# Two first projections back to back on TensorE, and the down weights' high part behind the copies of the sums on ScalarE

## The reference

```python
x = L0_attn_x                                    # (1, 2048, 512) float32
xn = _layernorm(x, axis=-1)
s = _L0_attn_ref(xn, Wq, bq, Wk, bk, Wv, bv)     # q: 16 x 32 heads, k and v: 16 x 8 heads
g = _silu(_L0_ffn_ref(xn, ln_w, gate_w, up_w, down_w))
x = x + s * g

# in _L0_ffn_ref (inner size 1792)
nx = x * jax.lax.rsqrt(mean(square(x)) + RMS_EPS) * ln_w
g = jnp.einsum('bsh,ih->bsi', nx, gate_w)
u = jnp.einsum('bsh,ih->bsi', nx, up_w)
return jnp.einsum('bsi,hi->bsh', jax.nn.silu(g) * u, down_w)
# in _L0_attn_ref, for each token by itself, between its 16 rows d and e
scores = jnp.einsum('bsdh,bseh->bsde', q, k) / sqrt(16)
out = jnp.einsum('bsde,bseh->bsdh', softmax(scores), v)
```

## Time and profile before

| | |
|---|---|
| median of 3 runs | 473.84 us (473.63 to 474.03) |
| the profiled execution's own time | 474.23 us |
| its span, first to last instruction | 472.4 us |
| PE busy | 465.8 us (99%) |
| DVE, ACT, POOL busy | 411.9 (87%), 243.7 (52%), 120.7 us (26%) |
| granted TensorE clock | 1.000, full speed (2.4 GHz) |

### The profile page before, as it was taken

The page is one execution under the profiler, slowest core; times in us unless marked ns, Lnnn a source line. Parts: engine busy times, 40 slices in busy tenths (PEclk is TensorE's granted clock), DMA queues, the critical chain, the costliest instruction groups (busy, mean ns, idle before and its releaser), DMA issues.

```text
span 472.4 us, 6230 instructions
## 1 busy us (share of the span) xinstructions
PE 465.8 (99%) x2130; PEld 391.6 (83%) x2130; DVE 411.9 (87%) x559; ACT 243.7 (52%) x417; POOL 120.7 (26%) x104
## 2 busy tenths in 40 slices
PE   8999999999999999999999999999999999999997
PEld 7899888888888878888888888888888888888886
DVE  6999778987898997989989898999998888888994
ACT  4784665568588888654112545225225335358102
POOL 2920213116221122233443101000011111127920
PEclk9999999999999999999999999999999999999999
DMA  8606997579779996573474649546656655514772
GB/s 269 253 2 239 356 370 263 224 263 259 213 246 307 291 369 248 188 268 133 135 231 167 218 188 366 207 182 223 222 201 223 223 200 201 200 44 135 288 247 89
DMA packets 44623, 105.70 MB, mean 224 GB/s; under 512 B 20272, under 2 KB 21808, under 8 KB 41264
## 3 DMA queue, kind: packets, MB, share of 16 engines
q1 hardware_dynamic: 44592, 105.31, 63.5%
HBM read 69.90 MB, written 35.40 MB: 223 GB/s over the span
## 4 chain that ended last, share of the span: by engine, by line
PE 95%; POOL 2%; DVE 1%; DMA 1%; ACT 0%; issue 0%; SPq 0%; POOLq 0%; DVEq 0%
PE gu_ps L558 18%; PE gu_ps L560 18%; PE gu_ps L561 18%; PE y_ps L700 8%; PE y_ps L701 8%; PE y_ps L702 8%; PE gu_ps L702 3%; PE gu_ps L700 3%; PE gu_ps L701 3%; PE gu_ps L729 2%; PE gu_ps L728 2%; PE gu_ps L733 2%; DMA xz<-x 1%; POOL h_kept L514 0%; PE y_ps L742 0%; PE gu_ps L579 0%
## 5 line engine op out<-in xcount | busy, mean ns | idle before, releaser
L558 PE MATMUL gu_ps<-z_hi,w_ops 128*128 128x512 f32 x378 | 147.2, 389 | 0.0
L560 PE MATMUL gu_ps<-z_lo,w_ops 128*128 128x512 f32 x378 | 147.1, 389 | 0.0
L561 PE MATMUL gu_ps<-z_hi,w_ops 128*128 128x512 f32 x378 | 147.1, 389 | 0.0
L501 POOL TENSOR_TENSOR h_lo<-h,h_hi 128x512 fp32r<-128x512 f32 x28 | 36.8, 1315 | 229.3 <-ACT h_hi L930 229.2
L558 PEld LDWEIGHTS gu_ps<-z_hi,w_ops 128*128 128x128 f32 x378 | 70.9, 188 | 15.2 <-ACT u L905 0.5
L561 PEld LDWEIGHTS gu_ps<-z_hi,w_ops 128*128 128x128 f32 x378 | 71.0, 188 | 14.8
L560 PEld LDWEIGHTS gu_ps<-z_lo,w_ops 128*128 128x128 f32 x378 | 70.9, 188 | 14.6
L700 PE MATMUL y_ps<-wd_ops,h_hi 128*128 128x512 f32 x168 | 65.6, 390 | 0.0
L701 PE MATMUL y_ps<-wd_ops,h_hi 128*128 128x512 f32 x168 | 65.5, 390 | 0.0
L702 PE MATMUL y_ps<-wd_ops,h_lo 128*128 128x512 f32 x168 | 65.5, 390 | 0.0
L930 ACT ACTIVATE h_hi<-h 128x512 fp32r<-128x512 f32 x28 | 17.6, 630 | 58.8 <-DVE h L1229 58.7
(11 more groups left out here) (143 smaller groups left out, 750.1 us busy)
## 6 DMA issues: line engine op xcount, KB each, us to landing
w_kept<-w_ops SPq DMA_DIRECT2D x13, 1792.0 KB, 6.4
w_ops<-w_kept SPq DMA_DIRECT2D x13, 1792.0 KB, 7.6
wd_ops<-wd_kept SPq DMA_DIRECT2D x35, 512.0 KB, 4.2
raw<-gate_up SPq DMA_DIRECT2D x30, 256.0 KB, 4.3
wd_kept<-wd_ops SPq DMA_DIRECT2D x14, 512.0 KB, 7.5
xz<-x SPq DMA_DIRECT2D x16, 256.0 KB, 6.0
raw<-down SPq DMA_DIRECT2D x14, 256.0 KB, 7.8
w_ops<-wd_kept SPq DMA_DIRECT2D x7, 512.0 KB, 7.0
```

The source lines that it names most:

```text
L501: pool.tensor_tensor(lo, src, hi.bitcast(F32), ALU.subtract).then_inc(h_lo_done, 1)
L558: pe.matmul(acc, w_h, z_hi[:, zi, c, :], start=start and c == 0, stop=False, skip_group_check=True)
L560: pe.matmul(acc, w_h, z_lo[:, zi, c, :], start=False, stop=False, skip_group_check=True)
L561: end = pe.matmul(acc, w_l, z_hi[:, zi, c, :], start=False, stop=c == 1, skip_group_check=True)
```

## The change

It adds and removes no instruction. It moves these, in the front of the program and in the groups 1 to 13 of the first pair:

```diff
@@ block.sync (SP)
             load_x(0, (JJ - 1,))
+            load_down(0)
             load_gate(1)
             load_up(1)
-            load_down(0)
             load_down(1)
@@ block.gpsimd (POOL)
             scale_tile(J)
+            scale_tile(J + 1)
             pool.wait_ge(bias_in, 48)
...
-            for j in range(J + 1, JJ):
-                scale_tile(j)
+            scale_tile(J + 2)
+            scale_tile(J + 3)
@@ block.tensor (PE)
             qkv_product(0)
+            qkv_product(1)
             second_tile(J)
-            qkv_product(1)
             second_tile(J + 1)
+            qkv_product(2)
             second_tile(J + 2)
-            qkv_product(2)
             second_tile(J + 3)
             qkv_product(3)
             gate1(0)
@@ block.scalar (ACT), the front
             z_tile(J + 1)
+            hi_wd(0)
             z_hi_tile(J)
             z_tile(J + 2)
+            z_hi_tile(J + 1)
             z_tile(J + 3)
             z_raw_tile(J)
-            z_hi_tile(J + 1)
             z_hi_tile(J + 2)
-            hi_wd(0)
@@ block.scalar (ACT), for g in range(1, NI)
                 hi_a(g + 1)
-                hi_wd(g)
                 take_u2(g)
                 silu0(g)
                 if g > 2:
                     hi_s(g + 1)
                 take_u3(g)
                 if g <= 2:
                     hi_s(g + 1)
+                hi_wd(g)
                 if g + 2 <= NI:
                     scale(g + 2)
@@ block.vector (DVE)
             z_lo_tile(J + 1)
-            z_lo_tile(J + 2)
             times_up0(0)
             qkv_take(2)
+            z_lo_tile(J + 2)
             z_lo_tile(J + 3)
+            qkv_take(3)
             t_add(0, 0)
-            qkv_take(3)
```

## The result

| | before | changed |
|---|---|---|
| median of 9 runs | 473.72 us (473.63 to 474.03) | 474.84 us (474.77 to 475.71) |
| ratio, 95% interval | | 1.0025 [1.0016, 1.0033] |
| the profiled execution: own time, span | 474.23, 472.4 us | 474.84, 473.1 us |

The account below looks back on a forecast made before the run. PE was taken to bound the kernel, busy 465.8 of 472.4 us. Front −0.79, group 11 +0.45 and group 13 +1.08 sum to +0.74, which on a median of 473.84 gives 474.6 us; range 472.8 to 475.4.

Parts of the forecast that it names:

- the front: Start of the kernel: `qkv_product(1)` fills PE's wait at 19.45, `gate1(0)` starts at 26.82 instead of 27.61; −0.79 us.
- group 11: DVE's chain delays `seed(12)` and so PE's `m6(12)`, recovered 0.29 included; +0.77 or +0.14, middle +0.45 us.
- group 13: POOL starts 0.06 before `lo_s(14)`, delaying the z operations, `times_up0(13)` and PE at `down_product(13)`; +1.08 us.
- the groups 1 to 10: `lo_s` meets POOL except in groups 9 and 10, but slack or a reduction covers it; no PE cost.
- the 0.29 of a stall: PE's loss before `m7(11)`, from ACT waiting 1.37 for a transfer before `hi_wd(11)`; the move takes it away.
- The price of a collision: A DVE operation with two SBUF inputs stands while POOL reads SBUF; 1.08 us each, bounds 0 and 1.3.
- The sign that the prediction named: In the profile after, L734 or L700 after group 13 waits for over 1 us in total.
- The DVE-first case: In group 11 DVE's product starts before POOL, which then holds `lo_s`; `m6(12)` +0.14 us against 179.16.
- The push by `hi_wd(10)`: It ends near 159.80, so ACT's `scale(12)` is 0.30 late, handed on to DVE's group 11.
- collisions cost nothing: Rival: POOL loses every race and DVE never stands on the path; −1.08, 472.8 us; chance 0.15.
- the lead of the front is lost to transfers: Rival: ACT stays at its old moments, PE waits for `seed(11)`, POOL is first in group 11; 475.4 us; chance 0.15.
- group 11 gives back its stall: Rival: `scale(12)` not pushed, DVE wins, `m6(12)` comes 0.12 sooner, group 13 pays; +0.17, 474.0 us; chance 0.15.

Follow-up runs that it names:

- j: The kernel before, unchanged, run again for a second profile; 473.58 us.
- k: The kernel before, unchanged, run a third time with a profile; 473.81 us.
- e: Changed kernel with POOL's `wd_lo_part(13)` held until both z operations of group 13 are done; 474.06 us, ratio 1.0 to the kernel before.
- d: Kernel before with `hi_wd(13)` alone moved to its new place; 474.96 us, ratio 1.0023 to the kernel before.
- c: Changed kernel with `hi_wd(13)` alone put back at its old place; 473.85 us, ratio 0.9999 to the kernel before.
- a: Changed kernel with `hi_wd(g)` at its old place in all 13 groups, so only the front changed; 473.37 us, ratio 0.9991 to the kernel before.
- i: Changed kernel with `hi_wd(13)` put back and POOL's `wd_lo_part(11)` held until `lo_s(12)` is done; 473.6 us, ratio 0.9988 to the kernel before.
- b: Kernel before with `hi_wd(g)` moved in groups 1 to 13, front as before; 475.52 us, ratio 1.0035 to the kernel before.
- f: Changed kernel with POOL in group 11 held until the product of the last reduction has run; 475.22 us, ratio 1.0023 to the kernel before.
- l: The changed kernel, unaltered, run again for a second profile; 474.33 us.
- g: Changed kernel with DVE in group 11 held before its third attention product until `wd_lo_part(11)` is done; 475.81 us, ratio 1.0036 to the kernel before.

## Why the prediction was right, and where its sizes were off

By the table, the change gives −0.56 in the front (32.71 against j's and k's mean of 33.27) and +1.64 in the groups (163.05 against 161.41), +1.08 in all; the medians say +1.12. The prediction's sum was −0.79 + 0.45 + 1.08 = +0.74. The terms measured −0.56 in the front, +0.38 in group 11, +1.11 in group 13, and +0.15 in the groups 1 to 10, which the prediction had put at nothing.

The sum took the 0.29 of a stall off the profiled execution's 474.23, and then took another 0.39 off to come to the median, which by j and k is the time of executions without that stall. So the 0.29 was counted twice, and the miss of 0.24 is of that size. The other errors nearly cancel, by luck: the lead of the front was put 0.23 too high and 0.15 was left out, and against them group 11 without its recovered stall was put at 0.74, where it measured 0.38.

**The front, −0.79 predicted, −0.56 measured.** The mechanism and nearly every moment were right: no gap at 19, POOL's scale ahead of the sum, a short wait for `qkv_take(0)`, `gate1(0)` at 26.81. That the moments agree to 0.02 is in part luck: this execution's transposes began 0.09 sooner. Counted from them, the third projection starts at 13.61, where 21.66 − 8.12 = 13.54 was forecast; the take ended in time, but PE started 0.15 behind it, where the forecast had 0.05. Against the predicted −0.79 the size was off in three small pieces. The changed kernel's start of 8.03 against 8.12 is none of the front's doing. The profiled execution of before was itself 0.05 slower in this stretch than j and k. And `gate1(0)` now starts behind its wait with a first matmul of 0.50 in place of 0.39, so that from it to `m1(1)` it is 40.74 − 26.81 = 13.93 in place of 41.44 − 27.61 = 13.83: 0.10, which I had counted for the projections, not here. So 26.81 − 27.61 = −0.80 becomes −0.80 + 0.09 + 0.05 + 0.10 = −0.56. The −0.57 of the front alone agrees.

**The price of a collision, 1.08 predicted.** Measured where POOL was first: 2.33 − 1.22 = 1.11 in group 13, and the blocked operation ended 1.09 behind POOL's end. The reason given is shown, not only argued: with the same instructions and POOL held back (e), 1.03 of the 1.11 went.

**Group 13, +1.08 predicted.** In the profiles 162.52 − 161.41 = 1.11 (d), and 163.05 − 161.94 = 1.11 (changed less c); in the medians +1.02 (d). All steps came at their places. The sign that the prediction named, PE waiting over 1 us in total, came as 0.72 + 0.11 + 0.28 = 1.11.

**Group 11, +0.45 predicted as the middle of +0.77 and +0.14.** The DVE-first case came true: `m6(12)` was forecast for 179.30 − 0.79 = 178.51 and came at 178.55. The push by `hi_wd(10)` was real (ACT's `scale(12)` starts at 159.09 after 159.50 in the earlier trace rows, 0.41 sooner, where PE leads by 0.70 since `m1(1)`: 0.29 late; the 159.50 had itself waited for a transfer, and beside k, where it had not, the push is 0.59). But the sum counted the 0.29 of PE's stall before `m7(11)` as recovered, and this is the term that was wrong: j and k, and a and d, which have the same order in group 11, show no such stall, even where ACT stands 0.8 or 0.9 for the transfer. Against such an execution the group costs 0.38 (c's 161.94 − 161.41 less the 0.15 below). The middle of the two cases and the stall that did not exist nearly cancelled, so the term looks right by luck.

**Groups 1 to 10, nothing predicted.** No PE gap appeared, and `lo_s` collided in half of them at no cost to PE, as forecast. But the matmuls at `m6(7)` (116.94) and `m6(11)` (165.97) follow each other a few hundredths more slowly, 0.07 and 0.08 in sum. This stands in i, c, b and the changed kernel (i's 161.58 − 161.41 = 0.17), and not in a or d, so it belongs to the high parts moved in these groups. ACT's seed and PE's first two matmuls there:

```profile
116.17 0.58 ACT L894 ACTIVATE gu_ps<-gu_ps 128x512 f32<-128x512 f32 x1
...
116.94 0.42 PE L559 MATMUL gu_ps<-z_hi,w_ops 128*128 128x512 f32 x1
117.20 0.39 PE L561 MATMUL gu_ps<-z_lo,w_ops 128*128 128x512 f32 x1
```

`seed(7)` ends at 116.75, 0.19 ahead of the matmul that waits for it, and the next step is 0.26 in place of 0.227. Wherever a seed ended 0.34 or more ahead, in all thirteen profiles, the steps are the usual ones; at 0.18 to 0.20 they lose 0.07 to 0.10, and at 0.14, as before `m6(12)`, 0.33 and more. So a late seed goes with the loss. That it comes from the moved high part through DVE is likely, but no run puts one of these groups back alone.

**The rivals.** That collisions cost nothing is refuted by d and e. That the lead of the front is lost to transfers is refuted by a, where it arrived whole. That group 11 gives back its stall needed `scale(12)` unpushed, and it was pushed; DVE won the race all the same.

## What to carry to other kernels

Before moving a small operation on an idle engine, ask what it releases and what that will run beside: here a copy of 0.6 us on ACT decided when POOL read SBUF, and so whether DVE stood still for 1.1 us just where PE waited for DVE. Run the second engine's work beside a reduction or an operation with a PSUM input, and gate it there by a wait if need be; in i PE lost nothing by such a wait. The wait has to end at the right operation: in f POOL waited too, but until `lo_s` stood next, and PE lost 0.28 more than with no wait at all. A meeting costs only where PE has no slack behind it: of the seven long `lo_s`, two brought PE a clear wait. Before a stall of a few tenths is taken as a gain to be recovered, profile the kernel a second time: one that hangs on a transfer's landing may be in one execution and not in the next.

## What the hardware showed that was not expected

- The blocking goes both ways, and is nearly complete in both. DVE behind POOL ended its own length less 0.13 behind POOL's end (1.09 for 1.22 in group 13, 1.08 in f, where POOL had started 0.37 sooner). POOL behind a DVE product ended at 173.84, 1.15 behind the product's end at 172.69, for an operation of 1.29 (group 11).
- An engine that was blocked takes its turn as soon as the other's operation ends, and then blocks in its turn: POOL, held by the product, held `lo_s(12)`, which began at 173.20, reached its end at 174.92, again 1.08 behind POOL's. One meeting made two delays.
- PE's first transposes began between 7.53 and 8.41 us in the thirteen profiles (the kernel before 7.87 to 8.12, the changed one 7.53 and 8.03), and the rest of the 470 us followed to within the differences of the table. The landing of x sets that start: in all thirteen it comes 1.67 to 1.69 behind the start of DVE's statistics of tile 3, and before the statistics of the tiles 2 and 3 DVE waits for a transfer of x for nothing in l (7.53) and for 0.91 us in i (8.41). This may be the larger part of the spread of the runs (1.19 among 27 of the kernel before), but only profiled executions show it, and the five runs of g lie within 0.09.
